# Experts' stage of a mixer and mixture-of-experts layer: other places (mod 256 bytes) for the operands of its matrix products, and a weight ring in two parts

## What is computed

```python
x = x + layernorm(mixer(layernorm(x)))           # x: 4 x 1024 x 256, fp32
x = x + layernorm(moe(layernorm(x)))
# moe, for xn of 4096 tokens x 256:
logits = xn @ router_w                            # 8 experts, the best 2 of each token, weights comb
for e in range(8):
    out += comb[:, e:e+1] * ((silu(clip(xn @ gate[e])) * (xn @ up[e])) @ down[e])   # 256 -> 1024 -> 256
out += the same form for one shared expert with 256 hidden
```

## The kernel before

| | stationary | moving |
|---|---|---|
| gate step | 64 (ring) | 0 (tokens) |
| down step | 128 (activations) | 64 (ring) |
| transposes | 64 to 112 (rows) | 32 (unit matrix) |

## Time and profile before

### The profile page before, as it was taken

How to read it: one execution, slowest core, us unless ns; L and a number is a source line. 1 busy time by engine, 2 the same in 40 slices (tenths; PEclk the granted TensorE clock), 3 DMA queues, 4 the chain that set the end, 5 groups by cost and what they waited for, 6 DMA issues and landing times.

```text
span 1186.7 us, 23315 instructions
## 1 busy us (share of the span) xinstructions
PE 1097.3 (92%) x7492; PEld 976.9 (82%) x7492; DVE 832.7 (70%) x2113; ACT 654.8 (55%) x1325; POOL 303.0 (26%) x358
## 2 busy tenths in 40 slices
PE   3989999999989998999999999999999999999940
PEld 2765776677767666999999999999999999999940
DVE  5986898897878766666666666666666666666645
ACT  6768866777665364444444444445444544444425
POOL 1142132633441534121221122122112211221224
PEclk9999999998989999999999999999999999999975
DMA  8655765973664789522331245555922367211239
GB/s 298 230 191 185 251 216 189 322 244 137 215 229 151 245 276 348 182 59 56 63 71 18 36 127 189 198 163 179 384 34 36 75 208 230 36 28 25 36 86 215
DMA packets 96617, 191.70 MB, mean 162 GB/s; under 512 B 8768, under 2 KB 59456, under 8 KB 96576
## 3 DMA queue, kind: packets, MB, share of 16 engines
q1 hardware_dynamic: 80160, 170.38, 41.7%
q0 software_dynamic: 16416, 20.85, 10.2%
HBM read 295.62 MB, written 86.41 MB: 322 GB/s over the span
## 4 chain that ended last, share of the span: by engine, by line
PE 80%; DVE 7%; issue 4%; DMA 3%; SPq 2%; ACT 2%; POOL 2%; ACTq 0%; DVEq 0%; POOLq 0%
PE bank L1337 12%; PE bank L464 12%; PE bank L1339 12%; PE bank L1338 12%; PE bank L1350 6%; PE bank L1348 6%; PE bank L1349 6%; PE bank L458 4%; PE bank L459 4%; PE bank L460 4%; PE bank L1325 1%; DVE xr L1478 1%; DVE a_cum L869 1%; DMA e_raw<-w_e 1%; POOL xs_scratch L1144 1%
## 5 line engine op out<-in xcount | busy, mean ns | idle before, releaser
L1337 PE MATMUL bank<-h_hi,w_both 128*128 128x256 f32 x936 | 268.2, 287 | 0.1
L1287 POOL DMA_INDIRECT acc_scratch<-cv,ids x78 | 126.9, 1627 | 551.4 <-DVE cv L1426 510.8
L1447 DVE TENSOR_SCALAR cv<-bank 128x256 f32<-128x256 f32 x312 | 132.1, 423 | 191.4 <-PE bank L1339 191.4
L1338 PE MATMUL bank<-h_hi,w_both 128*128 128x256 f32 x936 | 261.0, 279 | 0.0
L1339 PE MATMUL bank<-h_hi,w_both 128*128 128x256 f32 x936 | 260.9, 279 | 0.0
L1397 ACT ACTIVATE cv<-cv 128x256 f32<-128x256 f32 x312 | 130.3, 418 | 231.8 <-DVE cv L1447 231.7
L1389 ACT ACTIVATE h_lo<-cv 128x256 fp32r<-128x256 f32 x312 | 130.0, 417 | 114.8 <-DVE cv L1454 114.8
L1338 PEld LDWEIGHTS bank<-h_hi,w_both 128*128 128x128 f32 x936 | 176.6, 189 | 0.0
L1337 PEld LDWEIGHTS bank<-h_hi,w_both 128*128 128x128 f32 x936 | 176.4, 188 | 0.4 <-issue 0.3
L1339 PEld LDWEIGHTS bank<-h_hi,w_both 128*128 128x128 f32 x936 | 176.6, 189 | 0.0
L1454 DVE TENSOR_TENSOR cv<-bank,cv 128x256 f32<-128x256 f32 x312 | 132.4, 424 | 47.5 <-ACT cv L1397 39.2
(11 more groups left out here) (227 smaller groups left out, 2395.6 us busy)
## 6 DMA issues: line engine op xcount, KB each, us to landing
w_both<-w_split SPq DMA_DIRECT2D x228, 768.0 KB
xs_hi<-w_split SPq DMA_DIRECT2D x38, 768.0 KB
xs_lo<-w_split SPq DMA_DIRECT2D x38, 768.0 KB
e_raw<-w_e SPq DMA_DIRECT2D x64, 384.0 KB
w_split<-e_high SPq DMA_DIRECT2D x64, 384.0 KB
w_split<-e_raw SPq DMA_DIRECT2D x64, 384.0 KB
u<-xs_scratch SPq DMA_DIRECT2D x40, 260.0 KB
x_in<-x SPq DMA_DIRECT2D x8, 512.0 KB
```

The lines of the kernel that those rows point to most:

```text
L1337: nc.tensor.matmul(out, e_hi[f][:, cols], xg_hi[:, par, c, :], start=c == 0, stop=False)
L1338: nc.tensor.matmul(out, e_hi[f][:, cols], xg_lo[:, par, c, :], start=False, stop=False)
L1447: nc.vector.tensor_scalar(gate[:, f % 4, :], gu_ps[f % 2][:, 0:G], CLIP, -CLIP, ALU.min, ALU.max).then_inc(clipped, 1)
```

## The change

The ring is cut in two: one place for the gate and up columns (GUW = 1024 words) and another for the down columns (512 words, D_AT = 16 words further). Each chunk is now fetched by two DMAs of two pieces per partition (2 x 2048 and 2 x 1024 bytes) instead of one DMA with one piece of 6144 bytes, and both count on the same semaphore, so PE waits for 32 instead of 16 per load. X_AT goes from 48 to 16 words, H_AT from 16 to 0. The rows get a place of 320 words for each 260 (ROWS_AT), so that all of them start alike, and `ident` is allocated in front of `zeros`. `w_both` grows by 256 bytes, so that what lies behind it keeps its place mod 256. As built, the stationary operands of gate steps, down steps and transposes all stand at 64 and the moving ones at 128: every distance is 192. In the mixer only `ident` (32 before, 128 now) has another place mod 256.

```diff
-X_AT, H_AT = 48, 16
+X_AT, H_AT, D_AT, R_AT = 16, 0, 16, 0
+ROWS_AT = 320
+GUW = 2 * 4 * P
...
-        w_both = sb("w_both", [P, 2 * W_COLS], F32R)
+        w_both = sb("w_both", [P, 2 * W_COLS + HALF // 8], F32R)
...
-        ring = [w_both[:, f * 2 * CW:(f + 1) * 2 * CW] for f in range(FC - 2)] + [flat(v[:, :, :])[:, 0:2 * CW] for v in (xs_hi, xs_lo)]
+        xs_flat = [flat(v[:, :, :]) for v in (xs_hi, xs_lo)]
+        d_base = (FC - 2) * GUW + D_AT
+        gu_ring = [w_both[:, f * GUW:(f + 1) * GUW] for f in range(FC - 2)] + [v[:, 0:GUW] for v in xs_flat]
+        d_ring = [w_both[:, d_base + f * 2 * D:d_base + (f + 1) * 2 * D] for f in range(FC - 2)]
+        d_ring += [v[:, GUW + D_AT:GUW + D_AT + 2 * D] for v in xs_flat]
...
+        halves = lambda v: v.bitcast(F32).rearrange("p (h c) -> p h c", h=2)
+
+        def chunk_parts(e, f):
+            split = w_s[e, f, :, :].rearrange("p (h c) -> p h c", h=2)
+            return split[:, :, 0:4 * P], split[:, :, 4 * P:CW]
+
         def load_chunk(g, f, e, new):
             sp.wait_ge(down_done, g * FC + f + 1)
-            sp.dma_start(w[f].bitcast(F32), w_s[e, f, :, :], cond=new).then_inc(loaded[f], 16)
+            gu, d = chunk_parts(e, f)
+            sp.dma_start(halves(w_gu[f]), gu, cond=new).then_inc(loaded[f], 16)
+            sp.dma_start(halves(w_d[f]), d, cond=new).then_inc(loaded[f], 16)
...
         def gate_up(g, par, f):
-            pe.wait_ge(loaded[f], 16 if isinstance(g, int) and g == 0 else g * 16)
+            pe.wait_ge(loaded[f], 32 if isinstance(g, int) and g == 0 else g * 32)
...
+        ident = sb("ident", [P, P])
         zeros = sb("zeros", [P, GT * D])
...
-        ident = sb("ident", [P, P])
```

More of the change, by code:

```diff
@@ L217, in mixer @@
         x1 = [by_tile(flat(v[:, :, :])[:, k * TC * D:(k + 1) * TC * D]) for v in (e_raw, e_high) for k in range(2)]
-        homes = (ring, quad(u_flat[:, 0:2 * GT * ROW]), quad(x_home[0]), quad(x_home[1]),
-                 u_flat[:, 2 * GT * ROW:2 * GT * ROW + DC * G].rearrange("p (c g) -> p c g", g=G),
+        homes = (gu_ring, d_ring, quad(u_flat[:, R_AT:R_AT + 2 * GT * ROWS_AT])[:, :, :, 0:ROW], quad(x_home[0]), quad(x_home[1]),
+                 u_flat[:, R_AT + 2 * GT * ROWS_AT:R_AT + 2 * GT * ROWS_AT + DC * G].rearrange("p (c g) -> p c g", g=G),
                  cv_flat[:, 0:4 * G].rearrange("p (i g) -> p i g", g=G),
@@ L1182, in experts @@
     LAG = 3
-    w, rows, xg_hi, xg_lo, xg_f, gate, hg_hi, hg_lo, y, acc, x1, small = homes
-    e_hi, e_lo = [chunk[:, 0:CW] for chunk in w], [chunk[:, CW:2 * CW] for chunk in w]
+    w_gu, w_d, rows, xg_hi, xg_lo, xg_f, gate, hg_hi, hg_lo, y, acc, x1, small = homes
+    gu_hi, gu_lo = [part[:, 0:4 * P] for part in w_gu], [part[:, 4 * P:8 * P] for part in w_gu]
+    d_hi, d_lo = [part[:, 0:D] for part in w_d], [part[:, D:2 * D] for part in w_d]
     ids = sb("ids", [P, 2, GT], I32)
@@ L1245, in first_weights @@
             for f in range(FC):
-                sp.dma_start(w[f].bitcast(F32), w_s[e, f, :, :]).then_inc(loaded[f], 16)
+                gu, d = chunk_parts(e, f)
+                sp.dma_start(halves(w_gu[f]), gu).then_inc(loaded[f], 16)
+                sp.dma_start(halves(w_d[f]), d).then_inc(loaded[f], 16)
         def others():
@@ L1336, in gate_up @@
                     cols = slice(at + c * P, at + (c + 1) * P)
-                    nc.tensor.matmul(out, e_hi[f][:, cols], xg_hi[:, par, c, :], start=c == 0, stop=False)
-                    nc.tensor.matmul(out, e_hi[f][:, cols], xg_lo[:, par, c, :], start=False, stop=False)
-                    i = nc.tensor.matmul(out, e_lo[f][:, cols], xg_hi[:, par, c, :], start=False, stop=c == DC - 1)
+                    nc.tensor.matmul(out, gu_hi[f][:, cols], xg_hi[:, par, c, :], start=c == 0, stop=False)
+                    nc.tensor.matmul(out, gu_hi[f][:, cols], xg_lo[:, par, c, :], start=False, stop=False)
+                    i = nc.tensor.matmul(out, gu_lo[f][:, cols], xg_hi[:, par, c, :], start=False, stop=c == DC - 1)
             i.then_inc(gu_done, 1)
@@ L1347, in down @@
                 out = down_ps[par][t][:, 0:D]
-                nc.tensor.matmul(out, hg_hi[:, f % 4, toks], e_hi[f][:, 4 * P:CW], start=f == 0, stop=False)
-                nc.tensor.matmul(out, hg_hi[:, f % 4, toks], e_lo[f][:, 4 * P:CW], start=False, stop=False)
-                i = nc.tensor.matmul(out, hg_lo[:, f % 4, toks], e_hi[f][:, 4 * P:CW], start=False, stop=f == FC - 1)
+                nc.tensor.matmul(out, hg_hi[:, f % 4, toks], d_hi[f], start=f == 0, stop=False)
+                nc.tensor.matmul(out, hg_hi[:, f % 4, toks], d_lo[f], start=False, stop=False)
+                i = nc.tensor.matmul(out, hg_lo[:, f % 4, toks], d_hi[f], start=False, stop=f == FC - 1)
             i.then_inc(down_done, 1)
```

## The result

| | before | changed |
|---|---|---|
| median of 5 runs each, in turn | 1181.77 us (1177.61 to 1184.26) | 1188.52 us (1188.03 to 1193.1) |
| ratio to before, 95% interval | | 1.0079 [1.0055, 1.0103] |
| profiled execution, span | 1188.74 us, 1186.7 us | 1193.1 us, 1191.0 us |
| experts' stage in it, first to last product | 673.0 us | 681.5 us |

The change costs 0.8% by the ratio, 6.5 to 12.2 us by its interval; the two medians are 6.8 us apart. Forecast were 1165 us and faster. The median lies inside the range, at its upper edge, but the time moved the other way, and it is the rival "Slower" that came about.

The account below looks back on a forecast made before the run. The prediction took PE's start-to-start spacing in the experts' stage, 116.2 ns on average, as the bound. Spacing -17, first load +2 and reloads +1.5 gave -13.5 us from 1178.47, so 1165 us, range 1143 to 1189.

Parts of the forecast that it names:

- rival "Slower": Experts' stage: distance 192 holds every run at 118 ns or higher, 1189 to 1208 us; chance 0.20.
- Term 1: Experts' stage: one distance for all pairs lets every product run stay at 113.5 ns spacing, -17 us.
- rival "The place does not matter": Experts' stage: operand places leave the spacing alone, only DMA terms remain, 1182 us; chance 0.17.
- rival "Products reach the floor": Experts' stage: products reach the transposes' spacing, 109 to 111 ns, -41 us, 1144 us; chance 0.15.
- Term 2: First weight load: extra packets delay the queue, so PE's wait for group 2's rows grows, +2 us.
- Term 3: Weight reloads at the seven expert changes: extra packet time makes PE wait 0.2 us each, +1.5 us.
- Term 4: Second issue of chunks not reloaded, wider rows' place and moved unit matrix: no cost.

Follow-up runs that it names:

- e1_split_only: Changed kernel with all operands back at the places of before, leaving only the two DMAs per chunk: 1184.39 us, ratio 1.0040 to before.
- m1_map: Separate small program, only product runs at 16 distances, entered from transposes or distance-0 products: 64 and 192 gave 117.8 ns behind transposes, 113.3 behind distance 0.
- m2_entry: Separate product program varying the transposes' operand places before runs at 64 and 192: 18 of 32 entries reached 113.3 ns at 64, 3 of 32 at 192.
- m3_waits: Separate product program in the layer's order with waits on reached semaphores, 16 transpose places: 113.4 ns in 15 of 32 stretches at 64, 117.8 in all at 192.
- e2_uniform64: Changed kernel with X_AT and D_AT at 48, so every distance between products is 64 instead of 192: 1181.73 us, ratio 1.0007 to before.
- e6_entry128: Changed kernel with product distance 64, transposes' rows 192 and unit matrix 128 past the products' moving operand: 1169.26 us, ratio 0.9901 to before.
- e3_uniform0: Changed kernel with X_AT and D_AT at 0, so every distance between products is 0: 1198.47 us, ratio 1.0162 to before.
- e7_entry192: Changed kernel with product distance 64, transposes' rows and unit matrix both 192 past the products' moving operand: 1170.17 us, ratio 0.9909 to before.
- e4_turns: Changed kernel with product distance 64, transposes' rows at 192 and unit matrix at 0 past the products' moving operand: 1188.86 us, ratio 0.9988 to before.
- e8: e6_entry128 with split weights reordered in HBM, so each load of a chunk moves one piece per partition instead of two: 1168.59 us, ratio 0.9897 to before.
- e9: e1_split_only with split weights reordered in HBM, so each load of a chunk moves one piece per partition instead of two: 1183.64 us, ratio 1.0021 to before.
- e5_gate192: Kernel before, one DMA per chunk, with only X_AT 16 instead of 48, putting gate runs at 192: 1192.86 us, ratio 1.0032.

## Why the prediction was wrong

**Term 1, the spacing (-17 us; measured +6.2, changed against e1_split_only).** The step that failed is the condition that the prediction put into its sum: "If one distance for all pairs lets each run stay at" 113.5. It does not let it. Products at 64 and at 192 have two lasting spacings, 113.3 and 117.8 ns (m1_map, m2_entry, m3_waits), a run keeps the one it has through gate and down steps, and uniform distances, at 64 as at 192, leave the choice to the transposes (e2_uniform64: 34 stretches to 45; changed: 5 to 73). The sizes of both were right: the group in the good state measures 16.77 us for 16.78, in the bad one 17.41 for 17.4. Wrong was which of them would hold. (By the rows the saving of a group is smaller than the sum says: 6 x 2.08 + 2 x 2.34 is 17.16, not 17.2, and less 16.78 that is 0.38 us or 15 us for the stage, not 0.43 and 17.)

The rows had the answer in them, read the wrong way round. I read the distances 128 and 0 between the old kernel's steps as the source of its slow first intervals, which they are (0.12 us each), and took their removal for the gain. But these transitions were also what brought gate runs back to 113.3, in six steps of eight: with them gone (e2_uniform64, changed) no run changes its spacing except at transposes. The old kernel pays three slow intervals per step for this repair; the changed one saves these and loses the repair. That alone costs nothing, as e2_uniform64 shows, which lost it too and came out even because half of its entries are good. The changed kernel is slower because 192 is entered well so rarely, in 5 stretches of 78. In e6_entry128 the transposes themselves enter in the good state, and no repair is needed. That is the gain the prediction hoped for: its stage is 15.1 us shorter than that of e1_split_only, which has the same DMAs, and 12.8 shorter than before's.

The rival "Slower" named "192 is the wrong side: it holds every run at 118". The number came true, 1189 us, but its mechanism only in part. 192 does not hold a run at 118 (16.77 us per group early on, 113.3 in m1_map); it is hard to enter well. It got 0.20 and should have had more: the prediction itself noted that 113.5 was seen only at 64 and that the entry might decide, and did not price an entry that repeats at each pair of transposes.

The rival "The place does not matter" fell with e3_uniform0 and e6_entry128, 2.6% apart with the same instructions. The Trainium skill's page "TensorE: Matmul & The Clock Gate" (Step-by-step: what each phase is for) says that loading the next weights takes no read bandwidth from the running matmul. By that alone one instruction would have one spacing, and here the traces disagree: 120.0 ns at distance 0 and 113.3 or 117.8 at 64 and 192. By what mechanism the places act, no run shows. The rival "Products reach the floor" fell with m1_map: of 16 distances and two entries none was below 113.3. What the transposes reach, 0.11 us, does not carry over to these products.

**Term 2, the first load (+2 us; measured +0.2).** PE's wait for group 2's rows went from 0.84 to 1.06 us:

```profile
485.21 0.33 PE L1342 MATMUL bank<-ident,u 128*128 128x128 f32 x1 [1.06 <-DMA u<-xs_scratch]
```

On SyncE's queue in the changed kernel, from the first weights on:

```profile
450.25 0.72 SPq L1262 DMA_DIRECT2D w_both<-w_split  x1
...
463.71 1.53 SPq L1263 DMA_DIRECT2D xs_lo<-w_split  x1
...
468.34 8.80 SPq L450 DMA_DIRECT2D xs_scratch<-pad  x8
...
482.44 0.39 SPq L1227 DMA_DIRECT2D u<-xs_scratch  x1
```

From the first load to the issue of the rows are 32.2 us (450.25 to 482.44), before 29.9 (456.73 to 486.64): +2.3 us, so the extra time of the queue was forecast rightly at 2.4. But the first load is issued 14.4 us ahead of the stage's first product (464.66) and not 11.9 as before, so the rows are issued 17.8 us behind that product, where it was 18.0. The step that failed is that PE's wait would grow by what the queue loses. Why the loads start earlier is open; all kernels with the split have it, 14.3 to 14.7 us.

**Term 3, the reloads (+1.5 us; measured +1.2 in three waits).** Near in size, and at 0.6 us at most each within the bound, but with some luck: the sum had PE ahead by the saved spacing, which it was not, and the same wait is 0.3 us in e1_split_only, 0.3 in e6_entry128 and 1.5 in e7_entry192. Together terms 2 and 3 show 1.5 us of waits for 3.5, yet the split by itself costs 4.7 us (95%: 2.4 to 7.1) and 2.3 in the stage. So their total was about right, but not for the reasons given.

**Term 4 (nothing)** had one mistake. The place of the unit matrix and of the rows was costed at nothing because they are only 152 products. They decide the spacing of the 5616 products: moving the rows by 128 bytes, and with them only one buffer that PE does not read (`xg_f`), takes e2_uniform64 (1.0007) to e6_entry128 (0.9901).

**What stays open.** Why a pair of transposes keeps or loses the good state, and why it does so in turns at one place (e4_turns), I can't say; nor why 192 reached 113.3 in five stretches of the changed kernel and behind distance 0 in m1_map, yet in none of 32 in m3_waits. That a wait at the transposes can flip it is strongly suggested by e6, e7 and e8 (five of ten such stretches at 117.8, six of the other 227), but some flips have no such wait, and it was not tried by itself. Whether the place counts against the moving operand of the product before or of the same product was not told apart, as both mixed runs read 116.7. Whether the split costs by its pieces or by its number of issues is open in the total time; in the stage e9's profile speaks for the pieces. The 2.4 us that e1 loses outside the stage, and the 2.5 that e9 still loses in all, have no cause shown.

## What to carry to other kernels

Measure start-to-start spacing by position behind each break, not busy time: a spacing that takes two values for one instruction is a state, and the question is then what sets it, not which value the place has. Before removing an irregularity because it costs a few intervals, ask what it restores. Rare instructions between long runs (here 152 transposes among 5600 products) can decide the speed of the whole run, so their places are worth as much care as those of the products.

## What the runs showed of the hardware

- fp32r products of 256 columns with a new 128x128 stationary operand each: 120.0 ns at distance 0 (mod 256), 113.3 or 117.8 at 64 and 192, 116.7 to 123.3 at the others (m1_map, last twelve intervals of each run), at a granted clock of 1.00. None at 109.
- Each of the two spacings at 64 and 192 lasts through stretches of 54 and 90 products, with waits on reached semaphores in between, and changes at transposes or where the distance does (m3_waits, e6_entry128, e5_gate192).
- A run that goes down to 113.3 mostly does so over about four intervals (on average 124, 116, 115, 114 behind the transposes of e6_entry128; 120, 122, 116, 114 behind the down steps of the old kernel). One that stays at 117.8 shows nothing of the kind.
- With 512 columns the place is worth 3% at most (227 to 234 ns), and the best is 0, which at 256 columns has 120.0 ns, among the longest spacings.
